# Work beside a long scan on one core: each step gets a visit on a grid, the 3x3 convolution is cut into smaller parts, and a third buffer of diagonals

## The reference, cut to what matters

```
out = silu(bn(einsum('oc,bchw->bohw', exp_w, x)))            # layer 0: 96 -> 576 channels
out = silu(bn(dwconv(out, einsum('be,eckl->bckl', rw, dw))))  # 5x5 depthwise, kernels mixed per sample
out = out * sigmoid(silu(mean(out) @ w1) @ w2)                # gates
x = x + bn(einsum('boc,bchw->bohw', wpw, out))                # 576 -> 96
xx, z = split(gn(x) @ W_in); xc = silu(dwconv3x3(xx))         # layer 1: 192 channels
x_dbl = xl @ W_x; delta = softplus(dt_r @ W_delta + b)        # xl: xc forwards and backwards
h = exp(dt * A) * h + (dt * u) * B;  y = sum_n(h * C) + D*u   # 784 steps, 768 rows x 16 states
x = x + (layernorm(y) * silu(z)) @ W_out
t = t + w2 @ ifft(relu(fft(relu(ln(t) @ w1)) * (r + 1j*i)))   # layer 2: mixer over all positions
t = t + W2 q8(relu(W1 q8(ln(t))))                             # quantized feed-forward (ffn0)
t = t + linear attention(ln(t));  t = t + ffn1(ln(t))         # layer 3
```

## Time and profile before

| | us |
|---|---|
| median of 3 runs (lowest to highest) | 25924.48 (25921.59 to 25940.24) |
| the profiled execution, its own time | 25920.02 |
| its span in the trace | 25918.3 |
| DVE busy in the span | 23299.7 (90%) |
| PE busy | 20594.3 (79%) |
| ACT busy | 12372.3 (48%) |
| POOL busy | 8447.7 (33%) |
| mean granted clock of PE | 0.835 of 2.4 GHz |
| loop of 62 samples, 710.1 to 25429.8 us | 24719.7, which is 398.7 each |

### The profile page before, as it was taken

The page is one execution under the profiler, slowest core; times in us unless marked ns, Lnnn a source line. Parts: engine busy times, 40 slices in busy tenths (PEclk is TensorE's granted clock), DMA queues, the critical chain, the costliest instruction groups (busy, mean ns, idle before and its releaser), DMA issues. The chain is left out here.

```text
span 25918.3 us, 375043 instructions
## 1 busy us (share of the span) xinstructions
PE 20594.3 (79%) x125002; PEld 8874.9 (34%) x125002; DVE 23299.7 (90%) x21779; ACT 12372.3 (48%) x17021; POOL 8447.7 (33%) x4999
## 2 busy tenths in 40 slices
PE   5778878787788887877888878778888787788786
PEld 2333333333333333333333333333333333333332
DVE  5999999999999999899999999999999999999997
ACT  2454444444544444445444454454444444544444
POOL 2333333333333333333333333333333333333331
PEclk8888888888888888888888888888888888888886
DMA  2222222222222222222222222222222222222222
GB/s 74 67 73 65 71 73 63 74 69 67 73 65 71 72 63 74 67 67 74 63 71 72 65 73 68 68 73 64 70 72 64 74 68 67 73 65 71 72 63 63
DMA packets 646792, 1791.26 MB, mean 69 GB/s; under 512 B 76999, under 2 KB 87059, under 8 KB 644760
## 3 DMA queue, kind: packets, MB, share of 16 engines
q1 hardware_dynamic: 624280, 1726.94, 23.0%
q10 hardware_dynamic: 20480, 38.29, 0.5%
HBM read 1707.39 MB, written 44.96 MB: 68 GB/s over the span
## 5 line engine op out<-in xcount | busy, mean ns | idle before, releaser
L1468 POOL TENSOR_TENSOR drive<-du,Bb 128x784 f32<-128x784 f32 x3072 | 5681.0, 1849 | 15616.1 <-DVE drive L1074 15616.1
L457 PE MATMUL scan_sum<-prod,fold 64*64 64x392 f32 x40960 | 6473.1, 596 | 2446.1 <-DVE prod L1074 2426.9
L457 PE MATMUL bank<-pad,dg 64*64 64x392 f32 x59008 | 7746.3, 515 | 171.1 <-POOL dg L1411 98.3
L825 ACT ACTIVATE decay_even<-delta,alog 128x784 f32<-128x784 f32 x3072 | 2816.0, 917 | 9434.8 <-DVE state L1243 9390.8
L1074 DVE TENSOR_TENSOR prod<-state,Cb 128x784 f32<-128x784 f32 x6144 | 6262.4, 1019 | 0.0
L1243 DVE TENSOR_TENSOR_SCAN state<-decay,drive 128x784 f32<-128x784 f32 x3072 | 5825.0, 1896 | 314.9 <-POOL drive L1468 118.2
L1243 DVE TENSOR_TENSOR_SCAN state<-decay_even,drive 128x784 f32<-128x784 f32 x3072 | 5500.5, 1791 | 142.6 <-ACT decay_even L825 33.6
L457 PEld LDWEIGHTS bank<-pad,dg 64*64 64x64 f32 x59008 | 3546.6, 146 | 3994.4 <-issue 3190.7
L457 PEld LDWEIGHTS scan_sum<-prod,fold 64*64 64x64 f32 x40960 | 1732.1, 152 | 5910.1 <-issue 3996.8
L1074 DVE TENSOR_TENSOR drive<-du,Bb 128x784 f32<-128x784 f32 x3072 | 2980.5, 970 | 52.0 <-issue 52.0
L825 ACT ACTIVATE decay<-delta,alog 128x784 f32<-128x784 f32 x3072 | 2865.9, 935 | 2.9 <-DVE delta L1074 1.2
(11 more groups left out here) (175 smaller groups left out, 16623.0 us busy)
## 6 DMA issues: line engine op xcount, KB each, us to landing
Bb<-bc_rows SPq DMA_DIRECT2D x2048, 392.0 KB, 3.7
Cb<-bc_rows SPq DMA_DIRECT2D x2048, 392.0 KB, 4.2
xin<-in_x SPq DMA_DIRECT2D x64, 294.0 KB, 4.3
x_kept<-xin ACTq DMA_DIRECT2D x64, 294.0 KB, 3.7
x<-x_kept SPq DMA_DIRECT2D x64, 294.0 KB, 2.9
out_dram<-t SPq DMA_DIRECT2D x64, 294.0 KB, 2.7
crossed<-pwm ACTq DMA_DIRECT2D x128, 96.0 KB, 2.1
delta<-in_x SPq DMA_DIRECT2D x8, 1176.0 KB, 7.6
```

The costliest lines, as they stand in the source:

```text
L457: return pe.matmul(out, lhsT, rhs, start=start, stop=stop)
L825: return act.activation(out, in_, f, bias=bias, scale=scale, **more)
L1468: pool.tensor_tensor(drive[:, j % 2, :], du[:, m, :], Bb[:, q % SLOTS, :], ALU.mult).then_inc(drive_r.sem, 1)
```

## The change

The places of nearly all steps are written anew. `TAIL_AT` becomes a table with one place for every step number of the tail, and many places are odd numbers, at which ACT has a visit (52 and 53, for instance, are two DVE visits, but 53 alone is one of ACT's). `BLOCK` goes from 10.2 to 10.0, turns stand 9.0 behind the start of a block in place of 9.2 (7.0 in the last block), and all places behind `GATE_AT` in the lead are new. The first `yield 4.0` of `post` on DVE becomes 5.0.

The 3x3 convolution yields four times per channel block (3, 2, 2 and 2 taps) in place of twice (5 and 4). For block b=1 each product is split into four on 64x64 tiles, which may run side by side. `DRING` is 3, so POOL may build a chunk's diagonals when the chunk three before has been used, and its places are 2.4 units ahead of the chunk. To make room, the quantized input xq of the ffn moves into a free quarter of work[4].

```diff
-DRING = 2
+DRING = 3
-BLOCK = 10.2
+BLOCK = 10.0
-GATE_AT = LEAD_AT + T0 * BLOCK
+GATE_AT = LEAD_AT + T0 * BLOCK - 2
-TAIL_AT = ((0, 9.8), (6, 17.0), (11, 21.8), (16, 26.8), (20, 36.8), (21, 38.3), (25, 44.5), (32, 50.5), (40, 58.0), (42, 60.0),
+TAIL_AT = {0: 10, 1.2: 11, 3: 12, 4: 15, 5: 16, 6: 17, 7: 18, 8: 19, 9: 20, 10: 21, 11: 22, 12: 23, 13: 25, 14: 26, 15: 28, 16: 29,
...
-    return LEAD_AT + BLOCK * t + 1.2 + 0.8 * (2 * c + h)
+    return LEAD_AT + BLOCK * t + 1.0 + (0.75 if t < T0 - 1 else 0.6) * (2 * c + h)
-    return LEAD_AT + BLOCK * t + 9.2
+    return LEAD_AT + BLOCK * t + (9.0 if t < T0 - 1 else 7.0)
-        xq = sb("xq", [C, L], F8)
+        xq = work[0:C, 4, :].bitcast(F8)[:, 3 * L:4 * L]
...
-                    for c, taps in enumerate((range(0, 5), range(5, 9))):
-                        yield GATE_AT + 14 + 3.2 * b + 1.2 * c
+                    for part, taps in enumerate((range(0, 3), range(3, 5), range(5, 7), range(7, 9))):
+                        yield GATE_AT + (18 + part, 24 + 0.7 * part)[b]
...
+                            for h in range(2):
+                                rows = slice(64 * h, 64 * h + 64)
+                                for copy in range(2):
+                                    last = mm(P[h][64 * copy:64 * copy + 64, 0:HALF], weights[rows, rows],
+                                              pad[b][rows, 14 * h + dy:14 * h + dy + 14, dx:dx + HW], start=tap == 0, stop=tap == 8)
...
-                yield 4.0
+                yield 5.0
...
-                        yield LEAD_AT - 2
+                        yield (LEAD_AT - 2, LEAD_AT - 1, LEAD_AT + 1)[q]
-                        yield max(chunk_at(q - DRING, 1) + 1.5, chunk_at(q) - 2.5)
+                        yield chunk_at(q) - 2.4
```

More of the change, by code:

```diff
@@ L578, in pre @@
                             pe.wait_ge(xc_r.sem, xc_r.at(i, 1))
+                        c = part // 2
                         q = CONV3 + 2 * b + c
[L580 removed]
+                        if part % 2 == 0:
+                            pe.wait_ge(diag_r.sem, diag_r.at(i, q + 1))
+                            if b == 1:
+                                alone()
                         for tap in taps:
                             dy, dx = tap // 3 + 1, tap % 3 + 1
[L583 to L584 removed]
@@ L585, in pre @@
-                        if c == 1:
+                            weights = dg[:, q % DRING, tap - CHUNK * c, :]
+                            if b == 0:
+                                last = pair(PP, weights, lambda h: pad[b][:, 14 * h + dy:14 * h + dy + 14, dx:dx + HW],
+                                            start=tap == 0, stop=tap == 8)
+                                continue
+                            for h in range(2):
[3 more added lines that the diff above has]
+                                              pad[b][rows, 14 * h + dy:14 * h + dy + 14, dx:dx + HW], start=tap == 0, stop=tap == 8)
@@ L593, in pre, with steps @@
                 last.then_inc(dbl_mm.sem, 1)
[L594 to L599, removed]
+                yield from steps(i, (0, 1, 2, 3), GATE_AT + 30, (0, 2, 3, 4))
+            def steps(i, ms, at, hops):
+                for m, hop in zip(ms, hops):
+                    yield at + hop
                     if m == 0:
@@ L791, in ahead @@
             def ahead(i):
-                yield from steps(i, 4, NK, 0.0, 1.6)
+                yield from steps(i, (4, 5), 0.0, (0, 1.6))
                 yield from lead(i + 1)
@@ L798, in _ @@
                 scan(i, Beside(tail(i - 1)), Beside(ahead(i)))
-            scan(NB - 1, Beside(tail(NB - 2)), Beside(steps(NB - 1, 4, NK, 0.0, 1.6)))
+            scan(NB - 1, Beside(tail(NB - 2)), Beside(steps(NB - 1, (4, 5), 0.0, (0, 1.6))))
             go_on([Beside(tail(NB - 1))], END)
@@ L901, in pre, with softplus @@
                 act.dma_start(sample_of(bc_dram[:, 1:, :], i), dbl[DR:DR + 2 * NS, :]).then_inc(bc_st.sem, 16)
[L902 to L907, removed]
+                yield from softplus(i, (0, 1, 2, 3), GATE_AT + 31, (0, 0.1, 2, 2.1), (4, 6))
+            def softplus(i, ms, at, hops, pairs):
+                for m, hop in zip(ms, hops):
+                    yield at + hop
                     if m == 0 and later(i):
@@ L914, in softplus @@
                     ac(two(du[:, m, :]), banks(PP), ACT.Abs, bias=bdl[:, KS[m]:KS[m] + 1]).then_inc(dl_a.sem, 1)
-                for p in range(first, end, 2):
-                    yield at + hop * (end - first - 1) + 0.2 + 1.2 * ((p - first) // 2)
+                for p, hop in zip(ms[::2], pairs):
+                    yield at + hop
                     exponentials()
```

66 lines of the change are left out of this document (31 added, 35 removed), and 5 rows, old and new, of the table TAIL_AT.

## The result

The changed kernel takes 25575.87 us (median of 4 runs, 25565.03 to 25588.78) against 25923.03 (4 runs): 347 us less, ratio 0.9865 with a 95% interval of 0.9848 to 0.9882. I had forecast 25,140, 785 us less. The direction was right and the time lies in the wide range given (24,600 to 25,750), but outside the forecast's own 24,900 to 25,450, and the gain is 0.44 of the one forecast.

What follows compares the result with a forecast made beforehand. DVE bounds the kernel, with 35.6 us of gaps per pass. Waits gone, 26.0, less new waits, 13.3, give -12.7 a pass, -787 us over 62 passes: about 25,140 us, own range 24,900 to 25,450, wide range 24,600 to 25,750.

Steps and rivals of the forecast that it cites:

- What bounds: DVE is busy in 90% of the span; the change can win only in its 35.6 us of gaps per pass.
- What goes: Sum of DVE's waits in the loop that the new places should remove: -26.00 us per pass.
- Norm behind a turn: ACT's turn and norm get a visit each, so DVE's wait at the norm's product goes: -3.85 us a pass.
- Attention's products: DVE's waits at attention's small products go, with their chain ahead of or between smaller convolution parts: -8.75 us a pass.
- POOL: A third buffer lets POOL build diagonals earlier, so DVE's waits for its drives go: -1.90 us a pass.
- Four cast pairs: DVE's casts at 52, 54, 88, 90 wait for ACT: 2.77 us a pair, 11.1 a pass; ffn0's first cast 0.2.
- The copy of the odd half: DVE's copy of the FFT's odd half has ACT's turn one visit ahead: 0.8 us a pass above today's 0.59.
- Tiles and PE: PE's 36 products on 64x64 tiles for 18 on 128x128, and its waits for ACT at four summations, costed at nothing.
- Gram: DVE's Gram copy, whose product waits for ACT's token copies: +1.2 us a pass, bounds 0 to 1.58.
- B: The waits go and the casts wait little, at 1.92 us a pair or nothing: 24,926 or 24,449 us; chance 0.2.
- D: Slower: PE stops for ACT, its clock falls and POOL's drives come late: 26,020 or 26,550 us; chance 0.1.
- C: Half of the gain behind PE stays away because PE is cold: 25,660 us, 25,500 to 25,850; chance 0.2.

Runs made afterwards that it cites:

- the combined versions: Changed kernel with casts one unit later plus the odd half's copy later, that copy and delta steps later, or TensorE's first inverse round later: 24680.44, 24692.74, 24681.10 us.

## Why the prediction was off, step by step

- **What bounds.** Right. DVE's busy time did not move, and all of the difference lies in its named waits.
- **What goes, 26.0 us a pass.** Right as a sum. Of the old waits, 27.0 without the copy's 0.6, there are left, outside the casts, 88.4 / 62 = 1.4 (L1372, L1276, L1088, xin and the drive in the waits above): 25.6 went. The t adds, of which I kept half, went altogether.
- **Norm behind a turn, 3.85.** Right in mechanism and size: 228 us came back when it was undone.
- **Attention's products, 8.75.** The size is right, the cause given was half wrong. I named the split beside the places; the split alone can be undone at no cost.
- **POOL, 1.90.** It went, but not by the third buffer: with two buffers no drive is late.
- **Four cast pairs, 11.1 us, and 0.2 for ffn0's first cast.** This is the step that failed first. It was mis-sized: the casts measured 16.3 against 11.3. The unit price (2.77) was right to 0.02 at three of the four pairs; at visit 88 it was 5.96 in the mean, because ACT came 3.4 us late from the delta work. I had bounded a pair at 3.85 and taken the value at which ACT is free. The list of ACT's steps at the visit before was there to be read. ffn0's first pair took 2.03 in the mean: "as a full visit lies between" looked at ACT alone, and ACT stood 5.82 us there for PE's product.
- **The copy of the odd half.** The second term that failed: 1.4 with the old wait, 4.4 measured. "Today 0.59, 0.8 more" had no derivation from PE's order. The 5.5 us of inverse FFT moved ahead of the expansion on which ACT's turn waits, and nothing in my sum followed that.
- **Tiles and PE, costed at nothing.** Right for the split and, within 86 us, for the tiles; no run shows the 0.46 us taken for a change of tile shape in the time. Wrong for PE's order, and this is what the three misses above have in common. PE does not stand ahead of DVE any more, but ahead of ACT: in the loop ACT's waits for PE at the pads went from 692.4 to 1222.3 us and at delta from 234.5 to 559.3, and DVE paid for them at a cast or at the copy.
- The two misses, 5.0 + 3.0 = 8.0 a pass, less 0.8 of terms that were better than forecast (Gram, t adds), are the 7.2 between 12.7 forecast and 5.5 measured.
- **Rivals.** B and D did not come: the casts wait in full, and no drive is late. C gave a time near the one measured (25,660), but by a mechanism that did not come: it has the waits of DVE on PE coming back, and PE ahead of L1074, of L1358, of xin and of L1326 left 1.2 of 16.9 us a pass. PE's lower clock did play a part, at another place: in the wdl products ahead of the late visit, where the granted clock is 0.50.

What stays open: how much of the 3.4 us of lateness at visit 88 is PE at the lower clock. The four wdl products took 2.98 us there and 1.58 at the upper level. ACT waited for two such groups, 3.07 us at 8512.60 and 1.40 at 8517.38; with 1.58 for each it would have come some 2.8 us earlier, and its own delta work would be the rest. That is an estimate from the rows of one pass, and no run separates the two. Nor are the differences between the sum of waits and the times in the combined versions followed up, nor why ffn0's first pair is steady in some versions and not in others.

## What to carry to other kernels

When two engines work through fixed lists, a consumer that stands right behind the event which lets the producer start pays the producer's visit up to its input: here two exponentials, an eviction and a bias, 2.75 us a pair. One unit more between them won 695 us, twice what the whole change had won. Before pricing such a wait as if the producer were free, list what it still has to do from the visit before, and what each of those steps waits for on a third engine.

## What was not expected of the hardware

PE's granted clock fell to the lower level at about 8503, in 1.67 us in which PE waited for DVE behind two fp8 products. It stayed at 0.50 up to 8520, though PE's records show it busy for 16.10 of these 17.00 us. It was back at 1.00 at 8520, when PE had just run out of work, and stood there for 3 us with 0.13 us of work (the windows above). The prediction's rival C has it that activity releases the lower level; in this stretch it came back only when the work had ended. The four products of 6x392 took 1.58 us ahead of the fall and 2.98 behind it (PE's timeline: start, us, operation, idle before, releaser):

```profile
8498.80 1.58 PE L459 MATMUL bank<-dwo,wdl 6*128 6x392 f32 x4
...
8503.29 1.57 PE L459 MATMUL scan_sum<-prod,fold 128*64 128x392 f32 x4 [1.67 <-DVE prod L1088]
8504.80 2.98 PE L459 MATMUL bank<-dwo,wdl 6*128 6x392 f32 x4
```

So a wait of PE that cost nothing by itself made the products behind it slower, and ACT, and through it DVE, waited for them. Other durations hardly moved between the kernel before and the changed one: an even scan 1.79 us in both, an odd one 1.90 and 1.91, the product behind a scan 1.02 and 1.01, ACT's decay_even 0.92 in both.
